# Two-expert tiles of 64-row halves in a mixture-of-experts kernel: 36 tiles in place of 39, and the per-tile bias and row weight fetched by ScalarE

## The reference, cut to what matters

```python
logits = xf @ gate_w + gate_b
top_val, top_idx = jax.lax.top_k(logits, 2)
gate_score = jax.nn.softmax(top_val, axis=-1)
comb = jnp.einsum('tk,tke->et', gate_score, onehot) * alpha[:, None]
for each expert e:                       # a scan in the reference
    h = gelu(xf @ w1[e] + b1[e])         # 256 -> 1024
    out += (h @ w2[e] + b2[e]) * comb[e][:, None]   # 1024 -> 256
x = x + tanh(g_ffn) * out
```

## Time and profile before

| | |
|---|---|
| median of three runs | 305.71 us (304.41 to 309.05) |
| the profiled execution's own time | 305.23 us |
| its span, first to last instruction | 303.5 us |
| mean granted TensorE clock, share of full speed | 0.917 |
| TensorE busy | 261.4 us, 86% |
| VectorE busy | 212.7 us, 70% |
| ScalarE busy | 178.5 us, 59% |
| GpSimd busy | 147.0 us, 48% |

### The profile page before, as it was taken

How to read it: one execution, slowest core, us unless ns; L and a number is a source line. 1 busy time by engine, 2 the same in 40 slices (tenths; PEclk the granted TensorE clock), 3 DMA queues, 4 the chain that set the end, 5 groups by cost and what they waited for, 6 DMA issues and landing times.

```text
span 303.5 us, 9536 instructions
## 1 busy us (share of the span) xinstructions
PE 261.4 (86%) x3275; PEld 245.3 (81%) x3275; DVE 212.7 (70%) x703; ACT 178.5 (59%) x494; POOL 147.0 (48%) x122
## 2 busy tenths in 40 slices
PE   2999818734799999999999999999999999999910
PEld 2999818634699989999999999999999999999900
DVE  3898799997898777686677668667876555555500
ACT  2143869696674766857766685776666545555400
POOL 2121128994524456673765464454576454444240
PEclk9995955855899999999999999999999999999985
DMA  6999999996414444458355535453444844552320
GB/s 186 323 375 376 380 373 378 374 329 205 110 40 72 71 72 71 74 83 78 58 104 75 88 55 94 81 83 69 74 67 75 85 79 72 86 81 28 37 30 4
DMA packets 46719, 40.94 MB, mean 135 GB/s; under 512 B 23025, under 2 KB 43250, under 8 KB 46546
## 3 DMA queue, kind: packets, MB, share of 16 engines
q1 hardware_dynamic: 38544, 29.62, 33.1%
q0 software_dynamic: 7488, 10.39, 23.1%
q10 hardware_dynamic: 642, 0.33, 0.4%
HBM read 26.10 MB, written 9.37 MB: 117 GB/s over the span
## 4 chain that ended last, share of the span: by engine, by line
PE 61%; DVE 13%; DMA 5%; issue 3%; ACT 3%; POOL 1%; DVEq 0%; POOLq 0%; ACTq 0%
PE bank L635 31%; PE bank L655 29%; DMA out_dram<-xn,add_at 4%; DVE wreg L1105 1%; DVE rows L1096 1%; ACT wreg L842 1%; DVE xs L1075 1%; DMA xs<-xrows,fetch_at 1%; ACT rows L919 1%; DVE earlier L1149 1%; DVE wreg L1352 1%; DVE gmark L1139 1%; POOL out_dram L1586 1%; DVE rows L1488 0%; ACT xTp L906 0%
## 5 line engine op out<-in xcount | busy, mean ns | idle before, releaser
L635 PE MATMUL bank<-xTp,wreg 128*128 128x128 f16 x1872 | 153.1, 219 | 1.4 <-ACT xTp L906 1.4
L655 PE MATMUL bank<-wreg,rows 128*128 x936 | 150.5, 273 | 0.5 <-DVE rows L1490 0.5
L635 PEld LDWEIGHTS bank<-xTp,wreg 128*128 x1872 | 128.7, 98 | 9.8 <-ACT xTp L906 1.7
L919 ACT ACTIVATE rows<-bank,maskbias 128x128 f32<-128x128 f32 x312 | 88.9, 371 | 39.9 <-PE bank L635 20.0
L1586 POOL DMA_INDIRECT out_dram<-xn,add_at x39 | 65.7, 1685 | 86.5 <-DMA out_dram<-xn,add_at 54.6
L655 PEld LDWEIGHTS bank<-wreg,rows 128*128 128x128 f16 x936 | 79.1, 98 | 4.5 <-issue 0.6
L1488 DVE TENSOR_SCALAR rows<-rows 128x512 f16<-128x512 f32 x78 | 36.0, 461 | 41.7 <-ACT rows L919 41.5
L1578 POOL DMA_INDIRECT xs<-xrows,fetch_at x39 | 48.0, 1232 | 23.0 <-issue 11.3
L1490 DVE SCALAR_TENSOR_TENSOR rows<-rows 128x512 f16<-128x512 f32 x78 | 54.0, 692 | 2.7
L927 ACT ACTIVATE xn<-xn,maskbias 128x256 f32<-128x256 f32 x39 | 20.0, 512 | 36.6 <-DVE xn L1479 36.5
L1352 DVE SCALAR_TENSOR_TENSOR wreg<-wreg x14 | 32.1, 2291 | 12.1 <-ACT wreg L842 10.4
(11 more groups left out here) (208 smaller groups left out, 232.1 us busy)
## 6 DMA issues: line engine op xcount, KB each, us to landing
wreg<-in_L_ffn_fc_w_dram SPq DMA_DIRECT2D x16, 1024.0 KB, 13.0
xrows<-rows SPq DMA_DIRECT2D x4, 528.0 KB, 6.3
xs<-in_x_dram SPq DMA_DIRECT2D x4, 512.0 KB, 9.1
out_dram<-xs SPq DMA_DIRECT2D x4, 512.0 KB, 8.8
xs<-in_L_ffn_fc_b_dram SPq DMA_DIRECT2D x1, 1024.0 KB, 6.1
xs<-xrows,fetch_at POOLq DMA_INDIRECT x39, 3.8
out_dram<-xn,add_at POOLq DMA_INDIRECT x39
xTp<-xs SPq DMA_TRANSPOSE x37, 3.7
```

Of the source, the lines that this page charges most:

```text
L635: mm = pe.matmul(put, w, xT[:, i % NX, x_part, k, :], start=(k == 0 and n == 0), stop=(k == KC - 1 and n == 2))
L655: mm = pe.matmul(yb, h, w, start=(c == 0 and n == 0), stop=(c == FC - 1 and n == 2))
L919: op = act.activation(h32[i % 2][:, f * P:(f + 1) * P], bank[2 * (i % 2) + half][:, c * P:(c + 1) * P], ACT.Gelu, bias=b1cur[:, i % NX, f: ...
```

## The change: what it does

An expert's count is now rounded to 64 rows. Its full tiles are what is left after an odd 64-row half is taken off; at most 71 halves exist, so 36 tiles hold them: 32 of one expert, and four mixed ones, tiles 25, 28, 31 and 34, whose two halves can belong to two experts. This does not depend on the data. In a mixed tile:

- the first layer runs 12 passes of 64 tokens per chunk, 6 for each half's weights, into the two halves of the chunk's columns; gelu runs 16 activations of 64 columns where there were 8 of 128;
- the second layer runs, per chunk, three pairs of passes, each with 64 stationary columns, one into rows 0 to 63 of the bank and one into rows 64 to 127, and all 8 chunks stand in a block after the next tile's first layer (`mixed_second`) and not between its chunks;
- the second half's weights are copied by VectorE to a fixed place, since both halves' places can't be held in registers: 4 copies of 128x1024 fp16 for the first layer (`keep_w1`, two tiles ahead) and 4 for the second (`keep_w2`, one tile ahead);
- bias and row weight are taken half by half, and the result is added by two indirect DMAs of 64 rows, the second after the first has landed.

The tables for halves are built in 14 steps on VectorE, beside tiles 5 to 18 (`odd_halves`), with seven small TensorE passes after tile 17. Experts can now follow closer on each other, and the units from the eleventh on are converted at tiles 16, 17, 19, 20, 22 and 23. `fetch` moves from VectorE to ScalarE, between `weigh(i - 2)` and `gelu(i, 1)`, with its register loads.

```diff
-    TILES = (2 * T - E) // P + E
+    H = P // 2
+    HALF_TILES = (2 * T + E * (H - 1)) // H
+    TILES = (HALF_TILES + 1) // 2
+    MIXED_AT, MIXED_STEP, MIXED = 25, 3, E // 2
+    mixed_of = {MIXED_AT + MIXED_STEP * m: m for m in range(MIXED)}
...
-        for r in range(2, E):
-            units_of_tile[(r - 1) * PER_RANK] = (2 * r,)
-            units_of_tile[(r - 1) * PER_RANK + 2] = (2 * r + 1,)
+        first_of_rank = (0, 4, 8, 12, 16, 19, 22, 25)
+        for k, i in zip(range(4, NU), (4, 6, 8, 10, 12, 14, 16, 17, 19, 20, 22, 23)):
+            units_of_tile[i] = (k,)
...  TensorE, fc1
+                if c == 0 and i in mixed_of:
+                    pe.wait_ge(w1_kept, mixed_of[i] + 1)
+                rows_each = P // len(ws)
+                for h, of_half in enumerate(ws):
+                    at = c % (FC // 2) * P + h * rows_each
+                    put = bank[2 * (i % 2) + part_f][:, at:at + rows_each]
...  TensorE, fc2
+                for n, (h_part, w_part) in enumerate(((hp, 0), (hp, 1), (lp, 0))):
+                    for h, of_half in enumerate(ws):
+                        at = slice(h * rows_each, (h + 1) * rows_each)
+                        mm = pe.matmul(yb[at, :], h_part[:, at], of_half[w_part],
+                                       start=(c == 0 and n == 0), stop=(c == FC - 1 and n == 2))
...
+            def mixed_second(i, ws):
+                for c in range(FC):
+                    fc2(i, c, fc2_operands(c, ws))
...  ScalarE
+            def fetch(i):
...
+                elif i % 4 == 0:
...
+                    experts_ahead[:] = nc.values_load_multi_w_load_instructions(
+                        te_i[0:1, i:min(i + 4, TILES)], engines=[mybir.EngineType.Activation], min_val=0, max_val=E - 1,
...
+                for bias, (_, e) in zip(biases, of_rows):
+                    act.activation(bias, b1T[:, bass.ds(e, 1), :].rearrange("p a f -> p (a f)"), ACT.Copy)
+                act.wait_ge(xg_in[i % NXG], (i // NXG + 1) * 16)
+                for at, e in of_rows:
+                    op = act.activation(wcur[at, i % NX:i % NX + 1], xg[at, i % NXG, bass.ds(e + W_COMB, 1)].bitcast(F32), ACT.Copy)
+                op.then_inc(cur_ready, 1)
...
+                if i + 1 < TILES:
+                    fetch(i + 1)
                 gelu(i, 1)
...  VectorE
+            def keep_w1(m):
+                if m == 0:
+                    v.wait_ge(w_lo, NU - 2)
+                    v.wait_ge(out_init, 16 * NG)
+                if m >= 1:
+                    v.wait_ge(fc1_ps, 2 * (MIXED_AT + MIXED_STEP * (m - 1)) + 2)
...
+                for part in range(2):
+                    for k in range(KC):
+                        c = slice(part * UNIT + k * F, part * UNIT + (k + 1) * F)
+                        op = v.tensor_copy(kept_w1[part][k], whalf[:, bass.ds(at[0], 1), c].rearrange("p a n -> p (a n)"))
+                op.then_inc(w1_kept, 1)
...
-                if i + 1 < TILES:
-                    fetch(i + 1)
...
+                if 5 <= i < 18:
+                    odd_halves(i - 5)
+                if i == 18:
+                    odd_halves(13)
                 for k in units_of_tile.get(i, ()):
                     if k >= 4:
                         weights_lo(k, unit_regions(k))
+                if i + 2 in mixed_of:
+                    keep_w1(mixed_of[i + 2])
+                if i + 1 in mixed_of:
+                    keep_w2(mixed_of[i + 1])
...  GpSimd, add_tile
+                    pool.indirect_dma_start(
+                        out=out[:, :], out_offset=bass.IndirectOffsetOnAxis(ap=add_m[:, 0, m:m + 1], axis=0),
+                        in_=y_sb[0:H, i % 2, :], in_offset=None, compute_op=ALU.add).then_inc(added, 16)
+                    pool.wait_ge(added, added_by(i) - 16)
+                    pool.indirect_dma_start(
+                        out=out[:, :], out_offset=bass.IndirectOffsetOnAxis(ap=add_m[:, 1, m:m + 1], axis=0),
+                        in_=y_sb[H:P, i % 2, :], in_offset=None, compute_op=ALU.add).then_inc(added, 16)
```

More of the change, by code:

```diff
@@ L629, in fc1 @@
                 if c % (FC // 2) == 0 and i >= 2:
[L630 to L636, removed]
+                    pe.wait_ge(gelu_done, 2 * (i - 2) + part_f + 1)
+                if c == 0 and i in mixed_of:
[4 more added lines that the diff above has]
+                    put = bank[2 * (i % 2) + part_f][:, at:at + rows_each]
+                    for k in range(KC):
+                        hi, lo = of_half[k]
+                        for n, (w, x_part) in enumerate(((hi, 0), (hi, 1), (lo, 0))):
+                            mm = pe.matmul(put, w, xT[:, i % NX, x_part, k, h * rows_each:(h + 1) * rows_each],
+                                           start=(k == 0 and n == 0), stop=(k == KC - 1 and n == 2))
                 if c % (FC // 2) == FC // 2 - 1:
@@ L891, in _ @@
             act.wait_ge(units_ready, 2)
+            act.wait_ge(first_ready, 1)
             first_two = nc.values_load_multi_w_load_instructions(
@@ L923, in gelu @@
-                op.then_inc(gelu_done, 1)
+                    for h, bias in enumerate(biases):
+                        at = slice(h * rows_each, (h + 1) * rows_each)
+                        op = act.activation(h32[i % 2][:, f * P:(f + 1) * P][:, at],
+                                            bank[2 * (i % 2) + half][:, c * P:(c + 1) * P][:, at], ACT.Gelu,
+                                            bias=bias[:, f:f + 1], scale=1.0 / (X_SCALE * W_SCALE))
+                op.then_inc(gelu_done, 1)
@@ L925, in weigh @@
+            experts_ahead = []
+            fetch(0)
             def weigh(i):
@@ new lines, in keep_w2 @@
+            def keep_w2(m):
+                if m == 0:
+                    v.wait_ge(w_lo, NU - 2)
+                if m >= 1:
+                    v.wait_ge(y_ps, MIXED_AT + MIXED_STEP * (m - 1) + 1)
+                for part in range(2):
+                    for n in range(2):
+                        c = slice(part * UNIT + n * F, part * UNIT + (n + 1) * F)
+                        op = v.tensor_copy(kept_w2[part][n],
+                                           whalf[:, bass.ds(kept_region[0], 1), c].rearrange("p a n -> p (a n)"))
+                op.then_inc(w2_kept, 1)
@@ L1491, in split @@
                                        in1=hhi[i % 2][:, c], op0=ALU.mult, op1=ALU.subtract).then_inc(lo_done, 1)
-            experts = []
-            experts_ahead = []
-            fetch(0)
+            experts = [[(slice(0, P), first_expert)] for i in range(PER_RANK)]
             first_lo(1, 0, (first_two[1], first_two[0]))
```

303 lines of the change are left out of this document (244 added, 59 removed).

## The result

The kernel after takes 307.87 us (median of four runs, 305.9 to 309.45) where the kernel before takes 305.26 in the same session: a ratio of 1.0093, 95% interval 1.0054 to 1.0131, so some 2.8 us slower, inside the 2% that count as no change. The forecast was 306 us and no change. Three tiles of 5.30 us are gone and nothing came of it. The profiled execution of after has a span of 306.0 us, against 303.5.

The account below looks back on a forecast made before the run. TensorE was taken to bound the tiles, at 5.30 us each. The terms -15.9 + 0.5 + 2.9 + 1.8 + 4.6 + 2.2 + 4.2 = +0.3 gave 305.5 us for the profiled execution, 306 as a median, range 298 to 313.

Parts of the forecast that it names:

- First layer of mixed tiles, +0.5: TensorE, four mixed tiles: 96 passes of 64 columns in place of 48 of 128 cost +0.5 us in all.
- Second layer of mixed tiles, +2.9: TensorE, four mixed tiles: paired half-array passes, priced from the attention's 0.139 us, cost 0.7 us per tile, +2.9 for four.
- the rival of halves one after the other: Second-layer halves run serially on TensorE: +2.6 us per mixed tile, 312 us; sign: second layer near 5.2 us; chance 0.17.
- Bias and row weight by ScalarE, 0: Two activations of 0.2 us each per tile move to ScalarE, lie in its waits and cost 0.
- Conversions moved forward, +1.8: Converting units at two tiles out of three makes TensorE wait 1.8 us for second-layer inputs at tiles 18 to 21.
- Copies, +4.6: Ahead of tile 25, TensorE waits 4.6 us for VectorE's second-weight copies, taken at 0.43 us each; later mixed tiles 0.
- the clock, +2.2: After the wait ahead of tile 25, TensorE's clock is at 1.2 GHz for 4.36 us, half lost: +2.2 us.
- Half adds, 3.5 each: Each mixed tile's two serial adds into the result take 3.5 us apiece, ends 2.2 and 4.5.
- Tail, +4.2: At the end, mixed tile 34's adds put the last add 8.4 us after TensorE's last pass: +4.2 us.
- The rival of cheap adds: Half adds at 3.05 us, copies at 0.33, clock holds, register loads free: 298 us; chance 0.2.
- That of copies at 1.06 us: VectorE's weight copies take 1.06 us each, every mixed tile waits 4 to 5 us: 325 us; chance 0.05.
- That of a dear step on ScalarE: A register load holds ScalarE 0.9 us, converted tiles are later, waits grow by 4: 310 us; chance 0.06.

Follow-up runs that it names:

- the second run: The kernel after with its four mixed tiles run as whole tiles of one expert; 0.9551 of the kernel before, 290.54 us.

## Why the prediction was right, and where it was not

The time and the class were right, and so was the account in outline: three tiles' gain eaten by the copies ahead of tile 25, the clock behind them and the serial half adds. That the time came out within 2 us is luck in part, since two errors of some 5 and 6 us cancel. Point by point:

- **Three tiles, -15.9.** Right; 15.4 measured alone.
- **First layer of mixed tiles, +0.5.** Right: a chunk of 64-column passes takes 0.68 us at full clock (starts at 219.98 and 220.66 in the trace) where a plain one takes 0.6625, 0.1 us a tile.
- **Second layer of mixed tiles, +2.9.** Wrong in size: it is nothing. The two passes of a pair start together and pairs follow 0.109 us apart, the lower of the two ends:

```profile
229.88 0.27 PE L730 MATMUL bank<-wreg,rows 128*64 x1
229.88 0.27 PE L730 MATMUL bank<-at_col,rows 128*64 128x256 f16 x1
229.98 0.27 PE L730 MATMUL bank<-wreg,rows 128*64 x1
229.99 0.27 PE L730 MATMUL bank<-xn,rows 128*64 128x256 f16 x1
230.19 1.01 PE L704 MATMUL bank<-xTp,wreg 128*128 128x128 f16 x15
```

  The nearest row, the fp32 attention at 0.139, was a bad guide, since it split rows and not columns. By the parallel tiles of the Trainium skill (TensorEngine Tiling (Array Packing), Key Properties) the term is 0, and the trace agrees with it. The drain at a switch of mode, which the same page of the Trainium skill has, shows as 0.1 us at most: 0.20 from the last pair to the next whole pass, against 0.109. The weight loads of 64 columns take 110 ns where whole ones take 98, and lie under the passes. The block of 2.74 us refutes the rival of halves one after the other, by its own sign of 5.2, without an experiment.
- **Bias and row weight by ScalarE, 0.** Not contradicted: 205 and 198 ns each, the 0.2 us that was taken; undone, the time is 0.8 us higher, known to 3.3.

```profile
L1046 ACT ACTIVATE maskbias<-b1T 128x8 f32 x40 | 7.8, 205 | 0.6 <-issue 0.4
```

- **Conversions moved forward, +1.8.** Not settled: one wait of 0.84 us, for tile 21's split, and 1.7 us for this, the table and the fetch together in the second run, with zero inside the intervals. The wait at 207.83 is no part of it: the second run, which has the same conversions, lacks it. What it waits for is open.
- **Copies, +4.6, and the clock, +2.2.** The place, the releaser and the mechanism were right, both sizes too high: 3.41 us and 1.35, 4.8 together; the run without the copies gives 4.5. In the first, the copies are paced at 0.33, the lower end, not 0.43, while the register loads took 0.7, not 0.4, which nearly cancels. What makes the wait shorter is on either side of it: counted from 207.35, where tile 23's passes end by their pace (207.02 + 0.33), its second gelu began 1.6 us later, not 2.4, and TensorE stood idle from 213.29, after 5.9 us, not 5.3. In the second, the clock held for 2.69 us of the wait and came back after 2.69 us of work, not 4.36.
- **Half adds, 3.5 each.** Near: the eight half adds of after are 3.38 (237.63 - 234.25) to 3.92 us from issue to the next issue, 3.69 in the mean.
- **Tail, +4.2.** This is the step that failed. "At the end, tile 34 is mixed: tile 33's add lands about 1.4 us after TensorE's last pass" set the price by the place of one mixed tile. The price of the half adds is 10.2 us, by the run with one add, and 9.5 without the copies, (0.9944 - 0.9633) x 305.3; it is paid wherever they stand. The step had a triple of tiles at 16.5 us of adds against 16.7 of TensorE, so that TensorE set the pace and only the end counted. Measured are 54.1 us of adds for three triples (234.25 to 288.39), 18.0 each, against 16.0 of TensorE (15.9 + 0.1, with nothing for the second layer). The halves are 7.4 of the 18.0, near the 7.0 taken; the two whole adds are 10.6, 5.3 each, not 4.75. That 4.75 came from the last four adds, when no row is fetched or transposed any more; in the middle of the tiles a whole add takes up to 7.2 us (246.29 to 253.47). The last add came 11.0 us behind TensorE's last pass, where some 8 was the prediction's own sign. The miss stayed hidden in the sum because the second layer (2.9), the copy wait (1.2) and the clock (0.85) were priced too high by 4.9, against 6.0 too little here.

The rival of cheap adds fell with the half adds at 3.69; its 298 us also doesn't come out of the terms that it names, which take 0.7, 2.2, 2.7 and 0.7 off 306 and leave 299.7. That of copies at 1.06 us fell with 0.33. That of a dear step on ScalarE, 4 us, fell with the run that undoes it.

## What to carry to other kernels

Where each transfer waits for the one before to land, the chain of transfers is an engine of its own: add it up over the whole stage, per tile, beside TensorE's sum, at prices taken from that stage and not from its quiet end, before taking work off TensorE. Splitting such a transfer in two saves little on each: here a half costs 3.69 us where a whole one in the quiet tail costs 4.7. In the chain of what ended last, the share that moves from PE to DMA is a hint at the new bound and no more: three tiles less alone moved it from 61% for PE to 48% for DMA. What decides is a run that changes one of the two and not the other, such as one add for two, or less work on TensorE.

## What the runs showed of the hardware

- An accumulating indirect add of 64 rows is issued in 1.42 us at the least and has landed 3.1 us after its issue began, in the median of after; one of 128 rows takes 1.56 us at the least to issue and lands after 4.0 us in the median, up to 6.4. Half the rows save 0.1 us of the issue.
- Passes on the two column halves of TensorE run beside each other even where the program issues three of one half and then three of the other: a block of 48 took 2.75 us so, and 2.74 in pairs.
- The same wait of 3.4 to 3.6 us cost differently much clock. In the kernel after the clock fell inside the wait and 2.69 us of work ran at 1.2 GHz; in the run with one add it fell inside it too, and 5.58 us did; in the run with the fetch on VectorE it fell 1.08 us after the wait was over, and 3.41 us did. The windows of the run with one add, and of that with the fetch on VectorE:

```profile
211.15:213.32 2.17, 0.00 (x0) 0.00 (x0) 1.47 (x3) 0.00 (x0) 0.00 (x0) 1.00 0.13 40
213.32:214.56 1.24, 0.01 (x1) 0.04 (x2) 1.24 (x5) 0.00 (x0) 0.00 (x0) 0.50 0.55 106
214.56:220.14 5.58, 5.58 (x70) 4.84 (x71) 3.88 (x10) 3.14 (x14) 2.69 (x2) 0.50 0.33 44
```

```profile
213.86:217.46 3.60, 0.00 (x1) 0.04 (x2) 2.87 (x7) 0.00 (x0) 0.00 (x0) 1.00 0.43 93
217.46:218.54 1.08, 1.08 (x28) 1.03 (x29) 1.02 (x6) 0.13 (x1) 0.00 (x0) 1.00 0.08 15
218.54:221.95 3.41, 3.41 (x43) 2.87 (x40) 2.80 (x7) 2.09 (x9) 2.45 (x2) 0.50 0.18 15
```
